# A fused four-layer kernel: the first two norms computed from a token-major copy of the input, scaled by VectorE and GpSimd

## The reference, cut to what matters

```python
def _layernorm(x, eps=1e-05):
    m = jnp.mean(x, axis=-1, keepdims=True)
    v = jnp.var(x, axis=-1, keepdims=True)
    return (x - m) / jnp.sqrt(v + eps)

def _rmsnorm(x, w):
    return x * jax.lax.rsqrt(jnp.mean(x * x, axis=-1, keepdims=True) + 1e-06) * w

def _quantize(W):                       # ternary rounding of W1 and W2
    gamma = jnp.mean(jnp.abs(W))
    return jnp.clip(jnp.round(W / (gamma + 1e-05)), -1.0, 1.0)

x = L0_attn_x                           # (16, 256, 128)
xn = _layernorm(x)
x = x + _L0_attn_ref(xn, norm_weight, Wk, Wv, Wq, ...) + _L0_ffn_ref(xn, W1, b1, W2, b2)
# inside _L0_attn_ref: x_norm = _rmsnorm(xn, norm_weight), then k, v, q from x_norm
```

## Time and profile before

| | us |
|---|---|
| median of 3 runs (2128.51 to 2137.08) | 2136.36 |
| profiled execution: its own time | 2138.4 |
| profiled execution: span, first to last instruction | 2136.6 |
| PE busy in the span | 1807.6 (85%) |
| DVE busy | 1340.5 (63%) |
| ACT busy | 1026.4 (48%) |
| POOL busy | 383.6 (18%) |

### The profile page before, as it was taken

The page is one execution under the profiler, slowest core; times in us unless marked ns, Lnnn a source line. Parts: engine busy times, 40 slices in busy tenths (PEclk is TensorE's granted clock), DMA queues, the critical chain, the costliest instruction groups (busy, mean ns, idle before and its releaser), DMA issues.

```text
span 2136.6 us, 33764 instructions
## 1 busy us (share of the span) xinstructions
PE 1807.6 (85%) x11206; PEld 1218.2 (57%) x11206; DVE 1340.5 (63%) x5024; ACT 1026.4 (48%) x2474; POOL 383.6 (18%) x511
## 2 busy tenths in 40 slices
PE   6889578777777779898999888989899854999998
PEld 5465466666666646666577766545544542973333
DVE  3687888888888854587554676342211331559996
ACT  2433465566666633454543224544443223437787
POOL 0000100000000000141452002003144023506652
PEclk9999666666666757998999558989999967998999
DMA  2000200000000000000001400011023100624662
GB/s 117 1 13 13 52 20 20 26 20 20 20 20 20 14 35 1 1 2 7 0 1 38 124 1 1 1 50 28 15 20 60 79 17 32 120 69 85 111 115 39
DMA packets 95469, 76.26 MB, mean 36 GB/s; under 512 B 22336, under 2 KB 87232, under 8 KB 94528
## 3 DMA queue, kind: packets, MB, share of 16 engines
q1 hardware_dynamic: 87616, 65.57, 13.0%
q0 software_dynamic: 7680, 8.53, 2.2%
HBM read 49.12 MB, written 23.51 MB: 34 GB/s over the span
## 4 chain that ended last, share of the span: by engine, by line
PE 55%; DVE 29%; ACT 7%; issue 4%; another core or an unknown queue 1%; SPq 1%; DMA 1%; DVEq 0%; POOL 0%; PEld 0%; PEldq 0%; ACTq 0%; POOLq 0%
PE ps L212 51%; DVE sm L233 9%; DVE big L239 5%; ACT big L221 4%; DVE mw L233 3%; DVE big L225 2%; PE ps L216 2%; PE ps L2603 2%; DVE big L233 1%; DVE tmp L229 1%; ACT sm L221 1%; SPq L873 1%; DVE sm L229 1%; DVE ke L225 1%
## 5 line engine op out<-in xcount | busy, mean ns | idle before, releaser
L221 ACT ACTIVATE tmp<-ps,bi 128x512 f32<-128x512 f32 (+1 forms) x226 | 153.9, 683 | 211.6 <-PE ps L212 205.8
L212 PE MATMUL ps<-big,mw 128*128 128x512 f32 (+3 forms) x476 | 231.3, 593 | 14.9 <-DVEq L260 7.2
L221 ACT ACTIVATE sm<-sm 128x1 f32<-128x1 f32 x512 | 174.0, 340 | 106.6 <-DVE sm L233 96.0
L221 ACT ACTIVATE big<-ps,co 128x512 f32<-128x512 f32 (+1 forms) x296 | 173.9, 649 | 44.1 <-PE ps L212 39.8
L212 PE MATMUL ps<-big,co 128*128 128x256 f32 (+1 forms) x344 | 170.1, 629 | 25.3 <-DMA bi<-bia 11.6
L225 POOL TENSOR_TENSOR big<-big,co 128x512 f32<-128x512 f32 x32 | 40.1, 1275 | 724.2 <-ACT big L220 670.9
L239 DVE TENSOR_REDUCE big<-ps 128x2 f32<-128x512 f32 x256 | 159.2, 670 | 6.8 <-PE ps L212 6.7
L212 PE MATMUL ps<-big,tmp 128*32 128x256 f32 (+2 forms) x1180 | 130.5, 404 | 24.9 <-DVE tmp L229 19.5
L212 PE MATMUL ps<-ke 48*128 48x256 bf16 (+4 forms) x638 | 125.2, 309 | 30.7 <-DVE big L225 16.7
L212 PEld LDWEIGHTS ps<-big,mw 128*128 128x128 f32 (+1 forms) x476 | 93.3, 230 | 79.8 <-issue 47.4
L212 PE MATMUL ps<-ke,big 128*128 128x32 f32 (+1 forms) x608 | 84.2, 286 | 64.0 <-ACT big L220 64.0
(11 more groups left out here) (264 smaller groups left out, 3893.5 us busy)
## 6 DMA issues: line engine op xcount, KB each, us to landing
mw<-d_tab SPq DMA_DIRECT2D x32, 328.0 KB, 3.5
mw<-m SPq DMA_DIRECT2D x2, 4096.0 KB, 13.1
d_pt<-big SPq DMA_DIRECT2D x32, 192.0 KB
ke<-d_pt SPq DMA_DIRECT2D x72, 64.0 KB
big<-d_pt SPq DMA_DIRECT2D x72, 64.0 KB
mw<-d_pt SPq DMA_DIRECT2D x48, 64.0 KB
d_xs<-big SPq DMA_DIRECT2D x1, 2560.0 KB, 9.3
big<-d_xs SPq DMA_DIRECT2D x5, 512.0 KB, 6.5
```

The lines of the kernel that those rows point to most:

```text
L212: return e.matmul(out, lhsT, rhs, start=start, stop=stop)
L221: return e.activation(out, in_, f, bias=K("zero")[0:out.shape[0], :] if bias is None else bias, scale=scale, **kw)
```

## The change

The input is also given token-major (`xK`: 128 tokens on the partitions, 32 blocks of 128 features), and the first two norms are computed from it. VectorE takes mean and variance of a block by `bn_stats` and `bn_aggr`, ScalarE makes both square roots, VectorE the reciprocals. VectorE then writes each block minus its mean times the first factor into ke, and GpSimd the same with the second factor into `BIG[6]`, except every eighth block of these, which VectorE takes. TensorE transposes both by 128x128 blocks into PSUM. ScalarE copies the first to `BIG[2]` and the second, times the norm weight, to `BIG[3]`. The rounding of f1 and f2 moves into the loop, to steps 6 and 7 of 0 to 8. The identity alone is loaded first; the other constants come behind the biases, the feature-major input whole behind the early weights. Each engine's `loaded` stands behind its part of the stage. The numbers of `Norm` and waits on `ln_rcp` and the like are shifted by one norm; there is no other effect on later stages.

```diff
         def loads(e):
-            e.dma_start(CO[:, :], con).then_inc(s_c, 16)
+            e.dma_start(CO[:, 0:128], con[:, 0:128]).then_inc(s_id, 16)
             for i in range(4):
-                e.dma_start(BIG[1][:, 1024 * i:1024 * i + 1024], xT[:, 1024 * i:1024 * i + 1024]).then_inc(s_x[i], 16)
+                e.dma_start(BIG[4][:, 1024 * i:1024 * i + 1024], xK[:, 1024 * i:1024 * i + 1024]).then_inc(s_x[i], 16)
             e.dma_start(BI[:, :], bia).then_inc(s_b, 16)
+            e.dma_start(CO[:, 128:NCO], con[:, 128:NCO]).then_inc(s_c, 16)
             e.dma_start(MW[:, 2048:2048 + NE], early).then_inc(s_e, 16)
+            e.dma_start(BIG[1][:, :], xT).then_inc(s_xf, 16)
             e.dma_start(MW[:, 0:2048], m1).then_inc(s_m1, 16)
...
         def first_norm_pe(e):
+            e.wait_ge(s_id, 16)
+            for t in range(NT):
+                for w in range(2):
+                    if t > 1:
+                        e.wait_ge(*n0_cp(2 * (t - 2) + w + 1))
+                    for k in range(4):
+                        if w == 0:
+                            e.wait_ge(*n0_a(4 * t + k + 1))
+                        elif t % 2 == 0 and k == 3:
+                            e.wait_ge(*n0_c(t // 2 + 1))
+                        else:
+                            e.wait_ge(*n0_b(pool_blocks(t, k)))
+                        p = tr(e, PS[:, 2 * w + t % 2, 128 * k:128 * k + 128], XH3[w][:, 4 * t + k, :])
+                    p.then_inc(n0_turn.sem, 1)
...
+        def first_norm_act(e):
+            e.wait_ge(*n0_eps(3))
             for s in range(NT + 2):
                 if s < NT:
+                    e.wait_ge(*n0_var(s + 1))
+                    if s > 3:
+                        e.wait_ge(*n0_a(4 * (s - 3)))
+                        e.wait_ge(*n0_b(pool_blocks(s - 4, 3)))
...
+                    act(e, rst2(s)[:, 0:4], n0_agg[:, s, :, 1], ACT.Sqrt, bias=eps5).then_inc(n0_sqrt.sem, 1)
+                    act(e, rst2(s)[:, 4:8], n0_agg[:, s, :, 1], ACT.Sqrt, scale=1.0 + 1e-6, bias=eps11).then_inc(n0_sqrt.sem, 1)
                 if s > 1:
                     t = s - 2
+                    e.wait_ge(*n0_turn(2 * t + 1))
+                    act(e, BIG[2][:, sl(t)], PS[:, t % 2, :], ACT.Copy).then_inc(n0_cp.sem, 1)
...
+                    e.wait_ge(*n0_turn(2 * t + 2))
+                    act(e, BIG[3][:, sl(t)], PS[:, 2 + t % 2, :], ACT.Identity, scale=B("nw"), bias=zero0).then_inc(n0_cp.sem, 1)
+                if s in (3, 4):
+                    e.wait_ge(s_e, 16)
+                    act(e, TMP[:, 4 + s, :], W("f1" if s == 3 else "f2"), ACT.Abs, bias=zero0, accum_out=qs[:, s - 3:s - 2]).then_inc(tq_sum.sem, 1)
...
+        def first_norm_dve(e, dn):
...
             for s in range(NT + 1):
                 if s < NT:
+                    if s % 2 == 0:
+                        e.wait_ge(s_x[s // 2], 16)
+                    for k in range(4):
+                        e.bn_stats(n0_stat[:, s % 2, k, :], XK3[:, 4 * s + k, :]).then_inc(dv, 1); n_s = dn.up()
+                        if k:
+                            e.wait_ge(dv, n_s - (1 if k == 1 else 2))
+                            e.bn_aggr(n0_agg[:, s, k - 1, :], n0_stat[:, s % 2, k - 1, :]).then_inc(dv, 1); dn.up()
+                    e.wait_ge(dv, dn.n)
+                    e.bn_aggr(n0_agg[:, s, 3, :], n0_stat[:, s % 2, 3, :]).then_inc(n0_var.sem, 1)
+                if s:
                     t = s - 1
+                    e.wait_ge(*n0_sqrt(2 * t + 2))
+                    e.reciprocal(rst2(t), rst2(t)).then_inc(n0_rcp.sem, 1)
...
+                    for k in range(4):
+                        ts(e, XH3[0][:, 4 * t + k, :], XK3[:, 4 * t + k, :], n0_agg[:, t, k, 0:1], rst2(t)[:, k:k + 1], SU, MU).then_inc(n0_a.sem, 1)
+                    if t % 2 == 0:
+                        ts(e, XH3[1][:, 4 * t + 3, :], XK3[:, 4 * t + 3, :], n0_agg[:, t, 3, 0:1], rst2(t)[:, 7:8], SU, MU).then_inc(n0_c.sem, 1)
+                if s == 6:
                     quant_scale_dve(e, dn)
                     quant_round_dve(e, dn, "f1", 0)
+                if s == 7:
+                    quant_round_dve(e, dn, "f2", 1)
+            loaded(e)
+            e.wait_ge(s_xf, 16)
+
+        def first_norm_pool(e):
+            for t in range(NT):
+                e.wait_ge(*n0_rcp(t + 1))
+                for k in range(4 if t % 2 else 3):
+                    ts(e, XH3[1][:, 4 * t + k, :], XK3[:, 4 * t + k, :], n0_agg[:, t, k, 0:1], rst2(t)[:, 4 + k:5 + k], SU, MU).then_inc(n0_b.sem, 1)
+            loaded(e)
```

More of the change, by code:

```diff
@@ L138, with program @@
 Norm = namedtuple("Norm", "i m b src dst eps g be")
-def program(nc, xT, early, wts, bia, con, m1, m2, m3, r1, outT):
+def program(nc, xK, xT, early, wts, bia, con, m1, m2, m3, r1, outT):
     with ExitStack() as ctx:
@@ L348, in ln_dve @@
                         stt(e, q.dst[:, sl(t)], x[:, sl(t)], B(q.g), PS[:, 2 + t % 2, :], MU, MU).then_inc(ln_norm, 1)
-        n0_eps, n0_sqrt, n0_rcp, n0_bc, n0_xr, tq_sum, tq_ps = sems("n0_eps n0_sqrt n0_rcp n0_spread n0_rms tq_sum tq_ps")
-        qs, eps11 = small(8), small(1)
+        n0_eps, n0_var, n0_rcp, n0_a, n0_c = signals("vector", 3, 8, 8, 32, 4)
+        n0_sqrt, n0_cp, tq_sum = signals("scalar", 16, 16, 2)
+        n0_turn, tq_ps = signals("tensor", 16, 1)
+        n0_b, = signals("gpsimd", 28)
@@ L355, in rst2, with pool_blocks @@
+        qs, eps11, eps5, zero0 = small(8), small(1), small(1), small(1)
+        XK3 = BIG[4][:, :].rearrange("p (b d) -> p b d", b=32)
+        XH3 = [BIG[i][:, :].rearrange("p (b d) -> p b d", b=32) for i in (5, 6)]
+        n0_agg = TMP[:, 0, 0:256].rearrange("p (t k x) -> p t k x", k=4, x=2)[:, 0:NT]
+        n0_stat = TMP[:, 1, 0:48].rearrange("p (i k x) -> p i k x", i=2, x=6)
         def rst2(t):
             return RST[:, 8 * (t % 4):8 * (t % 4) + 8]
+        def pool_blocks(t, k):
+            return 4 * t - (t + 1) // 2 + (min(k, 2) if t % 2 == 0 else k) + 1
@@ L358, in first_norm_pe @@
         def first_norm_pe(e):
+            e.wait_ge(s_id, 16)
[12 more added lines that the diff above has]
+                    p.then_inc(n0_turn.sem, 1)
+                if t == 3:
+                    e.wait_ge(s_c, 16)
+                    e.wait_ge(*tq_sum(2))
+                    mm(e, PS[:, 6, 0:2], K("one"), qs[:, 0:2]).then_inc(tq_ps.sem, 1)
@@ L365, in first_norm_pe @@
                 if s > 1:
                     t = s - 2
[L367 to L383, removed]
-                    e.wait_ge(tq_sum, 2)
-                    mm(e, PS[:, 6, 0:2], K("one"), qs[:, 0:2]).then_inc(tq_ps, 1)
@@ L389, in first_norm_act @@
+            loaded(e)
+        def first_norm_dve(e, dn):
+            e.memset(eps11, 1e-11).then_inc(n0_eps.sem, 1)
+            e.memset(eps5, 1e-5).then_inc(n0_eps.sem, 1)
+            e.memset(zero0, 0.0).then_inc(n0_eps.sem, 1)
             for s in range(NT + 1):
                 if s < NT:
[L391 to L394 removed]
@@ L2952, in _ @@
             st = Count()
+            first_norm_pe(e)
             loaded(e)
-            first_norm_pe(e)
             barrier(e, st.up())
@@ L3023, in _ @@
             st = Count()
-            loaded(e)
             first_norm_act(e)
@@ L3166, in _ @@
             gn = Count()
-            loaded(e)
+            first_norm_pool(e)
             e.wait_ge(stage_end, after("first"))
@@ L3240 @@
     arrays = {
+        "xK": f["L0_attn_x"].reshape(NB, NC, C, 128).transpose(0, 2, 1, 3).reshape(128, T),
         "xT": f["L0_attn_x"].reshape(NB, NC, C, 128).transpose(3, 1, 0, 2).reshape(128, T),
```

63 lines of the change are left out of this document (17 added, 46 removed).

## The result

The changed kernel took 2106.79 us (median of four runs, 2104.12 to 2114.62) where the kernel before, run beside it, took 2136.72: ratio 0.9879, 95% interval 0.9851 to 0.9907. The forecast was 2124.5, with a range of 2115 to 2132. Faster was right, the size was not: 29.9 us instead of 11.9. Two later comparisons of the same two kernels gave 0.9914 (0.9886 to 0.9941) and 0.9889 (0.9865 to 0.9912). The profiled execution's own time is 2109.13 us, its span 2107.3, where before had 2138.4 and 2136.6.

The account below looks back on a forecast made before the run. The first stage was taken as loading (11.6 us), some 34 us paced by TensorE and a VectorE tail. Its end, 29.3 + 6.4 + 3.6 = 39.3 us instead of 51.15, saves 11.9: 2124.5 us, range 2115 to 2132.

Parts of the forecast that it names:

- full waits: First stage: VectorE's scalings wait out whole GpSimd instructions, 0.92 us more a tile, 6.4 us in seven tiles; chance 0.45.
- term 3: GpSimd and VectorE scaling side by side in the first stage: GpSimd 0.52 us per instruction, VectorE held up 6.4 us.
- term 1: Loading at the kernel's start: first part of the input used at 4.5 us, later loads hidden at no cost.
- term 2: VectorE's steps in the first stage: first reciprocal at 7.6 us, 21.7 us more to tile 7's reciprocal, at 29.3.
- row at 1293.35: Earlier trace: a tiny VectorE instruction took 0.31 us instead of 0.17 beside GpSimd's new kind of instruction, a 0.14 wait.
- third rival: First stage: GpSimd's queue of 28 instructions sets the end, passing 51.15 us from 1.50 us each; 2138.5 us, chance 0.03.
- mild sharing: First stage: VectorE and GpSimd hardly block one another; end at 32.9 to 35.8 us, total 2118 to 2121, chance 0.33.
- slow form: First stage: GpSimd's two-scalar instruction takes 0.8 us rather than 0.52; end at 46.1 us, total 2131, chance 0.17.
- rival of a late GpSimd: First stage: GpSimd's first call pays about 6 us for freshly loaded code, hidden up to about 9 us; no chance given.
- term 4: End of the first stage: TensorE and ScalarE don't lead; last reciprocal to barrier takes 3.6 us, GpSimd's scalings 2.5 of it.
- Sum: First stage: 29.3 + 6.4 + 3.6 = 39.3 us where the barrier opened at 51.15, 11.9 us less.

Follow-up runs that it names:

- the seven comparisons: All timed comparisons with the kernel before, variants of the changed kernel included; each saves 0.7 to 8.9 us more than its first stage does, 4.2 on average.

## Why the prediction was wrong

The direction was right, and so was the place of most of the gain; most of the sum's terms held. Two steps failed: the full waits of term 3, within the stage, and behind it the assumption that the later stages keep their time.

*Loading, term 1.* The first use came at 5.26, not 4.5: 0.8 us too early, because the small identity took until 2.6 us and the first part of the input 2.6 us from there, twice the 1.27 taken from the earlier trace rows. The early weights, the second part of the constants and the feature-major input (the ninth of ten transfers, not the seventh; landed at 21.6) cost nothing, as said.

*VectorE's steps, term 2.* Statistics 1.3 us, as in the earlier trace rows; first reciprocal 8.46 (7.6, by the late start and a table load behind it); reciprocal of tile 7 ended at 29.28, where the forecast had 29.3 without waits. That is partly luck: from the first reciprocal to there it took 20.8 us, 0.4 of waits included, instead of 21.7, and this made up for the start that came 0.9 late.

*GpSimd against VectorE, term 3: the step that failed in the stage.* "I take the full wait, since it was longer and its VectorE form is the very one used here." VectorE's form matched but GpSimd's did not, and GpSimd's decides: with a two-input product on GpSimd VectorE's four scalings took 1.5 to 1.6 us, with `tensor_scalar` 1.16 on average, alone 1.11. The 6.4 us were 0.4. The row at 1293.35, the only one with GpSimd's new kind of instruction, was the nearer one, and the text said so and set it aside. The Trainium skill, page "SBUF — State Buffer", section "Who interferes with whom", has the later of the two engines block for the whole instruction of the other. These runs do not agree: they show waits, but short ones and mostly on GpSimd's side (0.79 to 1.07 us).

*GpSimd's price, in the same term.* "2.6 ns a column, so 0.52 for 128" came from a line through 256 and 512 columns. It is 0.79 undisturbed and 0.85 on average. This made up for part of the first error: GpSimd became what sets the stage, by the mechanism of the third rival, "GpSimd alone sets the stage". Its formula, first reciprocal + 28p + 1.1, gives 7.9 + 23.8 + 1.1 = 32.8 with the measured 0.85; measured are 8.78 + 23.84 + 1.43 = 34.05. The rival was dismissed because its price would have had to pass 1.50 to make the stage longer than before. But a queue of 28 x 0.85 was the longest thing long before it was a loss, and no case of the forecast joined mild sharing with a slow form, which is what happened. The rival of a late GpSimd did not come up: its first scaling started at 8.78, 0.1 us after the reciprocal, and took 0.86 us.

*Tail, term 4.* From the last reciprocal 4.77 us instead of 3.6, of which GpSimd's four scalings are 3.25.

*Sum.* Stage end 34.05 instead of 39.3, 5.2 us less: about 6.0 less for the waits and 1.2 less for VectorE's steps, 0.9 more for the start and 1.2 more for the tail. With a gain of 17.1 in place of 11.9 the same sum would have given 2119.3 us, inside its range. What put the result below the range is the other step, "Whatever is saved here is saved in full: a barrier closes the stage, and the later stages keep their instructions and their order". The instructions and their order are kept, but their time is not: it scatters by 9 to 12 us from execution to execution in either kernel. In part it is luck of the first comparison, too: its four timings of the changed kernel have a median of 2106.79, the later ones 2118.24 and 2111.11.

*What is left.* Of the 29.3 us between the profiled spans, 17.1 are the stage (17.7 with the means of the table, 51.9 and 34.2), and 12.2 are the later stages, 21 of standstill among them with some of the rest against it. The three ratios have a mean of 0.9894, some 22.6 us. Between that and 17.7 lie 5 us; the table's means give 2.3 of them to the later stages, with a scatter larger than the difference, and the seven comparisons together 4.2. Where this gain arises stays open, whether the first stage has a lasting effect on the clock's pattern behind it too, and what caused the standstill: no second one was seen.

## What to carry to other kernels

Before charging a wait between VectorE and GpSimd, find the row with GpSimd's own form: here two tensors on GpSimd slowed VectorE by 35 to 45%, a scaling by 5%. Then price every queue that starts at one moment and runs unbroken (start + count x cost + tail) and compare it with the best case of the others, not only with the old time; the larger of the two is the stage. And when a kernel's later stages scatter by more than the effect, measure the changed stage by itself, in several profiles of both kernels, before explaining the difference of two spans.

## What the runs showed of the hardware

- GpSimd, 128 columns of f32, beside VectorE's work: copy 0.26 us, product of two tensors 0.37, `tensor_scalar` with one column 0.61, with two constants 0.66, with two columns 0.85 (0.79 undisturbed).
- A stage of identical instructions takes one of a few lengths some 2 to 3 us apart, by how much of it TensorE spends at the lower clock: stage 6 took 27.8, 30.0 or 33.0 us at a mean granted clock of 0.87, 0.78 or 0.71, all three in executions of the unchanged kernel before.
- VectorE once stood still for 6.4 and 16.8 us, and ScalarE for 6.3 and 15.4, beside indirect DMAs issued by GpSimd, with no releaser in the profile; VectorE went on at 1785.93, within 1 us after the last of these. In the 17 other profiles the same DMAs disturbed nobody.
